# Edge network of a graph kernel: second layer turned over, third layer applied per edge, bf16 scatter, destination rows by DMA

## The reference, cut to what matters

```python
edge = jnp.concatenate([x[source], x[target], edge_feat], axis=-1)   # 48 + 48 + 16
h = jax.nn.relu(edge @ W1 + b1)                                      # 128
h = jax.nn.relu(h @ W2 + b2)                                         # 128
message = h @ W3 + b3                                                # 48
msum = jax.ops.segment_sum(message, target, num_segments=n)
cnt = jax.ops.segment_sum(jnp.ones(...), target, num_segments=n)
update = msum / jnp.maximum(cnt, 1.0)[:, None]
```

## Time and profile before

| | |
|---|---|
| median of 3 executions | 11055.2 us (11045.51 to 11082.27) |
| the profiled execution | 11089.94 us |
| its span | 11088.1 us |
| TensorE busy | 9243.7 us (83%) |
| GpSimd busy | 4781.5 us (43%) |
| VectorE busy | 7022.9 us (63%) |
| ScalarE busy | 4528.6 us (41%) |
| mean granted TensorE clock | 0.925 of 2.4 GHz |

### The profile page before, as it was taken

How to read it: one execution, slowest core, us unless ns; L and a number is a source line. 1 busy time by engine, 2 the same in 40 slices (tenths; PEclk the granted TensorE clock), 3 DMA queues, 4 the chain that set the end, 5 groups by cost and what they waited for, 6 DMA issues and landing times. The chain is left out here.

```text
span 11088.1 us, 570048 instructions
## 1 busy us (share of the span) xinstructions
PE 9243.7 (83%) x240266; PEld 7632.4 (69%) x240266; DVE 7022.9 (63%) x16172; ACT 4528.6 (41%) x8837; POOL 4781.5 (43%) x4058
## 2 busy tenths in 40 slices
PE   5886766788888888888888886999999999958585
PEld 4665656777878778778787785666666666658485
DVE  7998978877777777777777776222222222267377
ACT  2333988943333333333333332443434344323132
POOL 0000000055555555555555554655555555335053
PEclk9998995599999999999999998999999999979598
DMA  3000014588888878878888885111111111048085
GB/s 27 0 0 0 0 18 193 227 275 271 281 268 270 283 260 284 267 262 280 270 275 265 272 279 167 21 20 20 20 20 20 20 20 20 12 161 283 23 274 167
DMA packets 479754, 1689.66 MB, mean 152 GB/s; under 512 B 166486, under 2 KB 227950, under 8 KB 477550
## 3 DMA queue, kind: packets, MB, share of 16 engines
q1 hardware_dynamic: 412926, 1632.87, 44.5%
q0 software_dynamic: 59776, 46.03, 2.8%
q10 hardware_dynamic: 6640, 4.93, 0.2%
HBM read 1521.16 MB, written 157.36 MB: 151 GB/s over the span
## 5 line engine op out<-in xcount | busy, mean ns | idle before, releaser
L1144 POOL TENSOR_TENSOR arena<-arena 128x768 f32<-128x768 f32 (+2 forms) x1800 | 2714.0, 1508 | 1938.6 <-DVE arena L1198 1931.8
L1128 ACT CAST arena<-banks 128x384 bf16<-128x384 f32 (+1 forms) x3600 | 1951.7, 607 | 3430.2 <-DVE banks L1194 3424.6
L1239 PE MATMUL banks<-arena 32*128 32x144 bf16 x118800 | 2300.8, 225 | 398.3 <-DVE arena L1166 287.1
L1227 PE MATMUL banks<-arena 128*128 128x48 bf16 x58800 | 2512.4, 184 | 1.4 <-issue 1.4
L1227 PEld LDWEIGHTS banks<-arena 128*128 128x128 fp8e4 x58800 | 2357.6, 96 | 16.7 <-issue 16.7
L1227 PE MATMUL banks<-xc,arena 128*128 128x48 bf16 x24500 | 2069.0, 185 | 328.2 <-DVE arena L1198 113.2
L1239 PEld LDWEIGHTS banks<-arena 32*128 32x128 bf16 x118800 | 1947.0, 92 | 519.8 <-DVE arena L1166 297.8
L1227 PEld LDWEIGHTS banks<-xc,arena 128*128 128x128 fp8e4 x24500 | 1917.0, 96 | 515.4 <-issue 309.2
L1198 DVE TENSOR_TENSOR arena<-banks,arena 128x384 f32<-128x384 f32 (+1 forms) x3600 | 1904.2, 567 | 354.2 <-ACT arena L1128 354.2
L1419 POOL DMA_INDIRECT f<-node_table,idx x1568 | 1580.9, 1008 | 1207.7 <-ACT idx L1434 759.4
L1194 DVE TENSOR_TENSOR banks<-banks,wslot 128x384 f32<-128x384 f32 (+1 forms) x3600 | 1874.7, 567 | 355.4 <-PE banks L1227 353.7
(11 more groups left out here) (315 smaller groups left out, 12206.7 us busy)
## 6 DMA issues: line engine op xcount, KB each, us to landing
arena<-onehots SPq DMA_DIRECT2D x1200, 768.0 KB, 4.4
arena<-onehots SPq DMA_DIRECT2D x300, 864.0 KB, 4.4
arena<-onehots SPq DMA_DIRECT2D x300, 800.0 KB, 4.3
onehots<-arena SPq DMA_DIRECT2D x100, 768.0 KB, 3.3
node_table<-xc SPq DMA_DIRECT2D x11, 2352.0 KB, 17.6
f<-node_table,idx POOLq DMA_INDIRECT x1568, 2.4
onehots<-arena SPq DMA_DIRECT2D x25, 864.0 KB, 3.5
onehots<-arena SPq DMA_DIRECT2D x25, 800.0 KB, 3.3
```

Source lines behind the costliest of these rows:

```text
L1128: m = nc.scalar.copy(as_bank(mp_b[:, b % 3, 0, tiles, :, 1]), bank)
L1144: nc.gpsimd.tensor_tensor(mp[:, b % 3, 2, 0:NTILE[b], :], mp[:, b % 3, 1, 0:NTILE[b], :], mp_b[:, b % 3, 1, 0:NTILE[b], :, 1], ALU.subtrac ...
L1227: m = nc.tensor.matmul(to, hot[:, i * P:(i + 1) * P], x_part, start=c == 0, stop=c == 2)
L1239: m = nc.tensor.matmul(banks[:, 4 + q, 0:3 * D], hot[rows, i * P:(i + 1) * P], mp_b[rows, b % 3, :, i, :, 1], start=b == 0 and i == 0, sto ...
```

## The change

It changes how the edge network computes the same thing.

- The second layer keeps W2 stationary and moves 512 columns in one matmul, so its result is hidden values by edges, and ScalarE adds its bias (`b2_c`); the bias matmul goes.
- The third layer is applied to each edge: 4 matmuls per half with the hidden columns (`h2T`, f32, 128x128) stationary and W3 (48 columns) moving. Its 48 f32 results are split into three bf16 parts by ScalarE (hi, mid) and VectorE (rest, lo), with a one beside the first part: 3 x 49 = 147 bf16 columns.
- The scatter multiplies bf16 one-hots by these 147 columns. VectorE reduces the three parts and adds 2 x 49 sums to `acc`. The pass over the nodes with W3 goes.
- The one-hots that stand with nodes on partitions are no longer turned on TensorE. SP loads the group's 1,024 destinations to all 128 partitions (`dst_rows`, 4 KB each) and VectorE compares them with the 128 nodes that begin at the group's first destination (`turn_dst`). SP loads those 128 node rows too, from a second copy of the node table in node order (`store_both`), so one matmul of 512 columns takes the place of two.
- A group may now span 128 nodes from its first destination, not 256 from a block's start; if one does not, the edge network is swept up to 98 times, not 49.
- The loop is written out for 4 groups (8 steps) and runs without emptying the pipeline.
- Preparation: first destinations are broadcast too, the parts of b2 are no longer made; at the start of a sweep VectorE computes all keys at once.

```diff
+in_order = nc.dram_tensor("node_rows", ((NB + 1) * P, D), F32).ap()
...
+    link(nc.vector.tensor_scalar(first_x[0:1, :], dst_i[0:1, :, 0], 0.0, None, ALU.max))
...
-    link(nc.vector.tensor_scalar(chk[:, 4:5], chk[:, 4:5], float(WIN) - 0.5, None, ALU.is_gt))
+    link(nc.vector.tensor_scalar(chk[:, 4:5], chk[:, 4:5], float(P) - 0.5, None, ALU.is_gt))
...
+sweeps1 = nc.values_load(sweeps_i[0:1, 2:3], min_val=1, max_val=NB)
...
-    nc.vector.memset(acc[:, :], 0.0)
+    nc.vector.memset(acc[:, 0:(NB + 1) * (D + 1)], 0.0)
+    nc.vector.memset(xc_raw[:, NB * D:(NB + 1) * D], 0.0)
...
+      act.dma_start(in_order.rearrange("(b p) f -> p b f", p=P), xc_raw[:, 0:(NB + 1) * D].rearrange("p (b f) -> p b f", f=D)).then_inc(r, 16)
...
-store_table(xc[:, :, :])
+store_both(xc[:, :, :])
...
+hot = l1_part(SLOTS * TILES * WIN // 2, BF16).rearrange("p (u k n) -> p u k n", u=SLOTS, k=TILES)
+hotT = l1_part(2 * HQ).rearrange("p (q e) -> p q e", q=2)
+parts = l1_part(HALF * P3, BF16).rearrange("p (q k f) -> p q k f", q=2, k=HALF)
+rest = l1_part(2 * HALF * D).rearrange("p (q k f) -> p q k f", q=2, k=HALF)
+dst_rows = l1_part(SLOTS * GROUP).bitcast(I32).rearrange("p (u e) -> p u e", u=SLOTS)
+xwin = l1_part(SLOTS * D).rearrange("p (u f) -> p u f", u=SLOTS)
...
+totals = [banks[:, 0:2, 0:P3], banks[:, 6:8, 0:P3]]
...
+def half_steps(eng, step, looped, last):
+  def turn(q0, g0, t0):
+    for i in range(QT):
+      step(i, lambda lag: (q0(i - lag), g0((i - lag) // 2), t0((i - lag) // QT)))
+  turn(lambda n: n, lambda n: n, lambda n: n)
+  with eng.Fori(0, looped) as t:
+    turn(lambda n: t * QT + (QT + n), lambda n: t * SLOTS + (SLOTS + n), lambda n: t + (1 + n))
+  for tt in range(looped + 1, NT):
+    turn(lambda n: tt * QT + n, lambda n: tt * SLOTS + n, lambda n: tt + n)
+  for i in range(last):
+    step(i, lambda lag: (2 * NG + i - lag, NG + (i - lag) // 2, NT + (i - lag) // QT))
...
+      def load_dst(g, u, p, free):
+        when(sp, hotT_ready, free)
+        sp.dma_start(dst_rows[:, u, 0:p * TILES],
+              dst[bass.ds(g * GROUP, p * TILES)].rearrange("(a e) -> a e", a=1).broadcast_to([P, p * TILES])).then_inc(dst_in[u], 16)
+      def load_xwin(g, u, free):
+        at = sp.value_load(first_at[0:1, bass.ds(g, 1)], min_val=0, max_val=NB * P - 1)
+        when(sp, transposed, free)
+        sp.dma_start(xwin[:, u, :], in_order[bass.ds(at, P), :]).then_inc(xwin_in[u], 16)
+      def load_attr(g, u, p, free):
+        sp.wait_ge(attr_placed, free)
...
+        load_dst(u, u, P, 0)
+        load_xwin(u, u, 0)
+        load_attr(u, u, P, u + 1)
...
+          load_dst(g, u, P, t * QT + (2 * u + 2))
+          load_xwin(g, u, t * QT + (2 * u + 2 + FREE))
+          load_attr(g, u, P, t * SLOTS + (SLOTS + u + 1))
...
+      def step(i, at):
+        q3, q2, q1, (q, g, t) = at(3)[0], at(2)[0], at(1)[0], at(0)
+        now, other = i % 2, (i + 1) % 2
+        if live(q3):
+          when(act, mapped, q3 + 1)
+          when(act, summed_q, q3 - 1)
+          nc.scalar.copy(parts[:, other, :, 0:D], psM).then_inc(hi_ready, 1)
+        if live(q2):
+          when(act, lin2, q2 + 1)
+          when(act, mapped, q2 - 1)
+          nc.scalar.activation(h2T[:, now, :], ps2, ACT.Relu, bias=b2_c[:, 0:1]).then_inc(h2T_ready, 1)
+        if live(q3):
+          when(act, rest_ready, q3 + 1)
+          nc.scalar.copy(parts[:, other, :, HD:HD + D], rest[:, other, :, :]).then_inc(mid_ready, 1)
+        if live(q1):
+          when(act, lin1, q1 + 1)
+          when(act, lin2, q1 - 1)
+          nc.scalar.activation(h1T[:, other, :], ps1, ACT.Relu, bias=b1_c[:, 0:1]).then_inc(h1T_ready, 1)
+        if live(q):
+          when(act, transposed, q + (FREE + 1))
+          when(act, lin1, q - 1)
+          nc.scalar.copy(rowsT[:, now, :], psT).then_inc(rowsT_ready, 1)
+          if now:
+            set_indices(g + SLOTS, i // 2)
+      half_steps(act, step, NT - 1, 3)
...
+      link(nc.vector.tensor_tensor(keys, dst_f[:, 0:NG, :], base[:, 0:NG].unsqueeze(2).broadcast_to([P, NG, TILES]), ALU.subtract))
+      link(nc.vector.tensor_scalar(beyond, keys, float(P) - 0.5, None, ALU.is_gt))
+      link(nc.vector.tensor_scalar(beyond, beyond, far[:, 0:1], None, ALU.mult))
+      link(nc.vector.tensor_tensor(keys, keys, beyond, ALU.add))
...
-      def make_onehots(g, u):
-        dve.wait_ge(summed_q, g * 2 + (SUMMED - 6))
-        nc.vector.tensor_scalar(dloc[:, u, :], dst_f[:, bass.ds(g, 1), :].rearrange("p a k -> p (a k)"),
-                    base[:, bass.ds(g, 1)], None, ALU.subtract).then_inc(window_step, 1)
-        blk = dve.value_load(base_blk[0:1, bass.ds(g, 1)], min_val=0, max_val=NB - 1)
-        nc.vector.tensor_copy(xwin[:, u, :, :], xc_raw[:, bass.ds(blk * D, 2 * D)].rearrange("p (h f) -> p h f", h=2))
-        dve.wait_ge(window_step, g + 1)
-        onehots(hot[:, u, 0:HALF, :], dloc[:, u, 0:HALF])
-        onehots(hot[:, u, HALF:TILES, :], dloc[:, u, HALF:TILES]).then_inc(hot_ready, 1)
...
+      def turn_dst(q, g, t, u, j):
+        when(dve, dst_in[u], t * 16 + 16)
+        when(dve, transposed, q + (FREE - 1))
+        mine = dst_rows[:, u, :].rearrange("p (e k) -> p k e", k=TILES)[:, HALF * j:HALF * j + HALF, :]
+        nc.vector.tensor_scalar(hotT[:, j, :].rearrange("p (k e) -> p k e", k=HALF), mine,
+                    row_w[:, bass.ds(g, 1)], None, ALU.is_equal).then_inc(hotT_ready, 1)
+      def make_onehots(q, g, t, u):
+        when(dve, attr_in[u], t * 16 + 16)
+        when(dve, transposed, q + 2)
+        nc.vector.tensor_copy(rows[:, u, :, D:KS], attr[:, u, :, :]).then_inc(attr_placed, 1)
+        when(dve, summed_q, q - 6)
+        nc.vector.tensor_copy(dloc[:, u, :], keys[:, bass.ds(g, 1), :].rearrange("p a k -> p (a k)")).then_inc(dloc_ready, 1)
+        when(dve, dloc_ready, g + 1)
+        for k in range(TILES):
+          m = nc.vector.tensor_scalar(hot[:, u, k, :], iota_b[:, :], dloc[:, u, k:k + 1], None, ALU.is_equal)
+        m.then_inc(hot_ready, 1)
+      def step(i, at):
+        q3, next_half, next_group, done = at(3)[0], at(-1), at(-2), at(7)
+        now, other = i % 2, (i + 1) % 2
+        if live(q3):
+          when(dve, hi_ready, q3 + 1)
+          when(dve, lo_ready, q3 - 1)
+          nc.vector.tensor_tensor(rest[:, other, :, :], psM, parts[:, other, :, 0:D], ALU.subtract).then_inc(rest_ready, 1)
+        if live(next_half[0]):
+          turn_dst(*next_half, (i + 1) // 2 % SLOTS, other)
+        if live(next_group[0]) and not now:
+          make_onehots(*next_group, (i // 2 + 1) % SLOTS)
+        if live(q3):
+          when(dve, mid_ready, q3 + 1)
+          nc.vector.tensor_tensor(parts[:, other, :, 2 * HD:2 * HD + D], rest[:, other, :, :], parts[:, other, :, HD:HD + D],
+                      ALU.subtract).then_inc(lo_ready, 1)
+        if live(done[0]) and now:
+          q, g, t = done
+          when(dve, summed_q, q + 2)
+          when(dve, folded, g)
+          nc.vector.tensor_reduce(gsum, totals[(i - 7) // 2 % 2].rearrange("p a (c f) -> p a f c", c=3), AX, ALU.add).then_inc(added, 1)
+          blk = dve.value_load(base_blk[0:1, bass.ds(g, 1)], min_val=0, max_val=NB - 1)
+          here = acc[:, bass.ds(blk * HD, 2 * HD)].rearrange("p (a f) -> p a f", a=2)
+          when(dve, added, g + 1)
+          nc.vector.tensor_tensor(here, here, gsum, ALU.add).then_inc(folded, 1)
+      make_onehots(0, 0, 0, 0)
+      turn_dst(0, 0, 0, 0, 0)
+      half_steps(dve, step, NT - 2, 6)
...
-            nc.tensor.matmul(ps2[:, :], ones_b[0:32, :], b2_parts[:, :], start=True, stop=False, skip_group_check=True)
...
+      def step(i, at):
+        q4, g4, q3, q2, q1, (q, g, t) = at(4)[0], at(4)[1], at(3)[0], at(2)[0], at(1)[0], at(0)
+        now, other = i % 2, (i + 1) % 2
+        if live(q3):
+          when(pe, h2T_ready, q3 + 1)
+          when(pe, rest_ready, q3)
+          for k in range(HALF):
+            m = nc.tensor.matmul(psM[:, k, :], h2T[:, other, k * P:(k + 1) * P], W3_s[:, :], start=True, stop=True)
+          m.then_inc(mapped, 1)
+        if live(q2):
+          when(pe, h1T_ready, q2 + 1)
+          when(pe, h2T_ready, q2)
+          nc.tensor.matmul(ps2, W2_s[:, :], h1T[:, now, :], start=True, stop=True).then_inc(lin2, 1)
+        if live(q1):
+          when(pe, rowsT_ready, q1 + 1)
+          when(pe, h1T_ready, q1)
+          nc.tensor.matmul(ps1, W1_s[:, :], rowsT[:, other, :], start=True, stop=True).then_inc(lin1, 1)
+        if live(q):
+          u = i // 2
+          if not now:
+            pe.wait_ge(gathered[u], t * (16 * TILES) + 16 * TILES)
+            pe.wait_ge(xwin_in[u], t * 16 + 16)
+            pe.wait_ge(attr_placed, g + (SLOTS + 1))
+          pe.wait_ge(hotT_ready, q + 1)
+          when(pe, rowsT_ready, q)
+          nc.tensor.matmul(psT[HC2:HC2 + D, :], xwin[:, u, :], hotT[:, now, :], start=True, stop=True, skip_group_check=True)
+          for k in range(HALF):
```

(45 more changed lines are left out.)

238 lines of the change are left out of this document (65 added, 173 removed).

## The result

The changed kernel takes 10317.15 us, the median of 4 executions (10312.97 to 10332.1), against 11053.16 us before (4 executions, 11045.51 to 11082.27): ratio 0.9328, 95% interval 0.9309 to 0.9348. The profiled execution took 10320.64 us. Forecast was 10300.

A forecast was written before the change was run, and what follows sets the result against it. TensorE bounds the edge network at 13.94 us a group; gathers take over at 10.63. Terms -666 - 95 - 4 + 9 + 2 = -754 from the profiled 11089.9 give 10336, less 35 for the median about 10300; range 10150 to 10600.

The forecast's parts named there:

- TensorE's bill: Edge network: TensorE's work after the change sums to 4.7 us a half, 9.4 a group, below GpSimd's 10.0.
- case 1: Edge network: gathers set the pace at 10.0 to 11.0 us a group, time 10300; chance 0.60.
- GpSimd 2084 us: Edge network: the same 1568 gathers, waits for indices becoming 0.30 us gaps, take 2084 us, 10.63 a group.
- The tail: End of the edge network: about 25 us for the last landing and the last five steps.
- Pass over the nodes: After the edge network: the pass goes, saving 94.6 us, counted as 95.
- Clearing: Before the edge network: clearing 4851 columns instead of 12771; the reload of x then ends last, a gain of 4 us.
- Preparation: Before the edge network: 8 small linked instructions come, 9 go, two f32 broadcasts come; 2 us more.
- Second store: Before the edge network: storing the second node table beside the first costs 9 us more (5 to 12).
- Destination loads: Edge network: SP's 512 KB destination loads, issued about three groups (30 us) ahead, cost nothing.
- case 3: Edge network: VectorE holds gathers back for all its work; one-hots alone +290 us, 10590, all of it 10940; chance 0.12.
- case 2: Edge network: TensorE still sets the pace, 11.2 us a group, 10410; sign: gathers waiting for ScalarE's indices; chance 0.20.
- case 4: Edge network: TensorE's clock falls to 1.2 GHz, 18.8 us a group, 11900; sign: clock under 0.9; chance 0.03.

The follow-up runs named there:

- half-gather runs: Only 4 of each group's 8 gathers, in the changed kernel (9976.4 us) and in the kernel before (10946.7 us), both on chip 3.
- v_late_rows: Changed kernel with the second table's store only started before the edge network, SyncE waiting for it before its first row load; 10370.0 us on chip 10.
- b_half_gathers: The kernel before with only 4 of every group's 8 gathers; 10946.7 us on chip 3, against 11202.9 for the kernel before beside it.

## Why the prediction was right, point by point

- **TensorE's bill**: 4.7 us a half foreseen, 4.72 found: third layer 0.87 (0.9), second 0.93 (0.96), first 0.95 (0.96), target rows 0.99 (0.93), turning 0.46 (0.46), scatter 0.52 (0.5). The upper bounds (0.25 a matmul, weight loads that don't hide) were not needed.
- **The bound changes hands** (case 1, 10.0 to 11.0 us a group): yes, 2069.7/196 = 10.56, by the waits in the trace; both half-gather runs agree, on another chip.
- **GpSimd 2084 us**: 2069.7 (1592.0 + 477.7). I had left 448.3 us of gaps as they were and added 182 of 0.30; the gaps came to 477.7 where I said 503, since the few gaps of up to 1.9 us of before are gone (the longest is 0.31). The gathers are 11 us longer, not equal.
- **The tail**: about 25 us; last gather at 8957.54, copy of the degrees at 8982.15, 24.6.
- **Pass over the nodes** -95: -94.5. **Clearing** -4: -2.0. **Preparation** +2: not seen; VectorE's copy before the clearing comes 0.7 us earlier, and a difference of that size can't be told from one execution to the next. **Second store** +9 (5 to 12): +13.6, the one term outside its bounds, since the two stores hardly overlap: apart they take 7.0 and 15.4 us to landing in v_late_rows, 22.4 in sum, and started together they held the stage back for 21.4 (6865.54 to 6886.92).
- **VectorE and ScalarE hidden**: 339 and 333 us of 700, 5.1 and 5.0 us a group, where I had 5.6 and 5.8. **TensorE idle**: about 1 us a group foreseen, (279.3 - 92.0)/195 = 0.96 found. **Destination loads** cost nothing: 512 KB land in 3.7 us.
- **The sum**: -754 foreseen, -769.4 found. The stage gave 19.7 more than foreseen: 14.3 in GpSimd's row (less in the gaps, more in the gathers), 2.7 because I ended the old stage at its last add and not at the copy of the degrees, the rest at the ends. The second store took 4.6 back and clearing 2.0; the 2 for preparation did not come. Median 10317 against 10300.

Two small slips of the working changed nothing: the 107 us of stretching before are 101 when counted from the gathers' median of 0.944 us and not 0.94, and the 12.1 us a group of case 3 are 10.0 + 1.9 = 11.9 by its own parts, so +249 and not +290 us.

Two things in it were wrong though the number was right.

**Which VectorE instructions stretch a gather.** "I charge VectorE only where a gather starts in a long two-input operation" held for the kernel before, where 101.4 of 102.4 us of stretch are in gathers that start during L175, but is false for the changed one: of its 112.1 us, 51.5 are in gathers that start during the comparison, a one-input operation on int32, and on chip 13 four fifths went when the comparison went. That the total was nearly unchanged was luck. The Trainium skill (SBUF — State Buffer, section Who interferes with whom) has two-input operations and the two-port modes contend, says that tensor_scalar can enter those modes, and spares a one-input operation only outside them. The comparison and the one-hots are both tensor_scalar operations, and no run here tells which mode either runs in, so the stretching by the comparison does not speak against that rule. Where the expectations of the two runs without the comparison forecast no change by it, they took it for granted that the comparison runs outside those modes. What is not borne out is the price that my third case put on the rule, that the bf16 one-hots hold the gathers back for their whole length: 1568 one-hots of 0.21 us are some 330 us, and on chip 13, together with all else that was left, they cost at most 12.

**That one chip stands for all.** The prediction treats 1.25 us a gather and prompt hand-overs as given. On chip 13 a group takes 14.9 us (2929.0/196) by waits that no case of mine contained, the whole kernel 11053.7 us, far outside 10150 to 10600. The forecast was right because the result was taken on a chip of the quick kind, and that is luck too. Two of its signs were on my list, gathers that wait for indices (case 2) and a clock under 0.9 (case 4), but in neither with this cause. The kernel before suffers less there, as I read it because its gathers were already interrupted each group by late indices. How much less can only be estimated, if all but the stage takes as long as in b_half_gathers: a span of 11201.1 less 8162.3 is 3039 us for its stage on chip 3, 258 more than on the result's chip. The changed kernel loses 834 on chip 13 (2929.0 against 2095.2).

## What to carry to other kernels

Work out each engine's bill from the distances between starts, and take the engine that comes next as the new floor. Here TensorE's cover of a tenth under that floor (9.44 of 10.56 us) was enough on two chips and not on three. Before edits are blamed for a surprise, run the unaltered kernel beside them on the same chip; here six experiments were at first read wrongly for want of it. A stage that rests on an unbroken row of gathers, with results passed between engines every microsecond, should be timed on more than one chip.

## What was not expected of the hardware

- Two kinds of chips, each chip visited once. On two (the result's and chip 10) ScalarE takes up the third layer 0.3 us after the start of TensorE's last record of it, beside an unbroken row of gathers. On three TensorE's semaphores change up to 15 us late after rows of gathers (94 of 223 hand-overs over 2 us late on chip 13), while those of the other engines change at once. The same three are faster ahead of the stage, which starts at 6753 to 6800 us of the span and not at 6876 to 6950.
- A comparison of 512 int32 with a stride of 32 bytes takes VectorE 0.68 us, with runs of 16 bytes 0.48.
- TensorE takes 1.91 us instead of 0.99 for an f32 matmul of 512 columns that are read with a stride of 16 bytes.
- An f32 matmul of 48 columns behind a 128x128 weight load takes 0.22 us at full clock, as half of its cost at 1.2 GHz had said.
